# Rotary partners by on-chip copies, values in 64 columns and another order at the entry of an attention, on one core

## The chip, the core and the metric

The kernel runs on one core of one Trainium2 chip. The core has five engines, each with its own queue of instructions in a fixed order: TensorE (PE in the profile; its weight loads are PEld), VectorE (DVE), ScalarE (ACT), GpSimd (POOL) and SyncE (SP), which here only issues transfers (DMA). They meet at semaphores: an instruction waits until a counter has reached a value, and adds to one when it is done. The metric is the time of one execution in device microseconds.

## The reference

Two layers on `x` (32 rows of 64 tokens, 128 wide) and a context of the same shape. The change touches the first attention, and SyncE's part of the mixture of experts that follows it.

```python
# layer 0, attention: 16 heads of 8; query from layernorm(x), key and value from ctx
q = proj(query, Wq, bq); k = proj(key, Wk, bk); v = proj(value, Wv, bv)
q = q * cos + rotate_half(q) * sin          # rotate_half: [-x2, x1] inside a head
k = k * cos + rotate_half(k) * sin
attn_w = softmax(einsum('bhqd,bhkd->bhqk', q, k) * scale)
out = einsum('bhqk,bhkd->bhqd', attn_w, v) -> [B, S, D] @ Wo.T + bo
x = x + tanh(g_xattn[0]) * out
# layer 0, experts: per row of x the two best of 8 experts (128 -> 512 -> 128, gelu), weighted
x = x + tanh(g_ffn[0]) * moe(layernorm(x))
# layer 1: attention by autocorrelation (Fourier transforms), then a gated MLP in fp4 steps
```

## The kernel before

Everything stays in on-chip memory. The 2048 tokens are 16 tiles of 128 tokens (two rows of the batch each); four tiles make a group, so there are four groups of keys and four of queries. Every engine's program is written out by hand, in the order in which it runs. There is no scheduler: the order of the code and the semaphore waits alone set what runs when.

**Entry of the first attention** (before the loop over tiles). For each group, `project` multiplies 512 tokens by a weight matrix, and again by the same matrix with its columns exchanged (`wk0r`, `wq0r`): within a head of 8, channel i of the second result is channel i xor 4 of the first. This second one is the rotary partner. VectorE multiplies the one by the table `cos` and the other by `sin` while it reads them from PSUM (L837), and GpSimd adds the two (L384, semaphore `rope_sum`). So it goes for the four groups of keys and for queries 0 and 1. Queries 2 and 3 (`late_projection` on ScalarE, `late_queries` on GpSimd) are copied out of PSUM raw and turned on GpSimd. The queries come from layernorm(x): VectorE takes the statistics (L250, L257), GpSimd the power -1/2 (L282), ScalarE or VectorE normalises (L270, L272), TensorE turns a group over (`turn`, L1218) and ScalarE copies it into `xt` (L545). `values` makes the values in 8 rounds of 8 products with 128 columns each. Of the 128, ScalarE keeps the half that belongs to the heads on its partitions (L541).

The keys of a group are spread into 8 blocks `kbd`, one for each pair of heads, with all the other channels zero: a multiplication with a column of `hmask` for each block. Blocks of group 0 are made by VectorE (L844) and ScalarE (L560), those of group 1 by ScalarE, and those of groups 2 and 3 by GpSimd (L376).

**Loop over tiles.** On TensorE, step t is: turn the probabilities of tile t over (L1292), scores of tile t+2 (`keys_queries`, L1279), turn the output of tile t-1 over (L1311), weigh the values of tile t (`weigh_values`, L1305), project the output of t-1 (L1315). VectorE takes the maximum (L858) and subtracts it (L866); ScalarE copies the turned probabilities (L587), takes the exponent (L582), and copies the turned output (L592), which L1315 waits for. At t = 9 VectorE also takes the statistics of the first 8 finished tiles.

**Experts.** 64 pairs of row and expert are sorted by expert into 36 tiles: 28 with two pairs, then 8 with one. For each, SyncE reads the expert's number from on-chip memory (L338), waits until the buffer is free (there are six, so tile j waits for the second product of tile j-6), and issues the copy of that expert's weights from `wall` into the buffer (L341). TensorE then runs `hidden` (L1472) and `second` (L1487).

SyncE's queue begins with all the loads. The last of them, `ctxN` and `wall`, are first used after the attention.

## Time and profile before

| what | before |
|---|---|
| three runs: median, lowest, highest | 269.43, 267.22, 270.42 us |
| profiled execution: time, span | 268.33 us, 266.5 us |
| busy: PE, DVE, ACT, POOL | 247.3, 185.1, 162.8, 129.6 us |
| granted TensorE clock | 1.00 |
| first scores (L1279), first weighing (L1305) | 26.19 us, 35.08 us |
| end of the loop over tiles, experts | about 92 us, 105 to 169 us |

The span is from the first to the last instruction; the time has 1.83 us more around it. The profiled execution lies 1.10 us under the median of the three.

### The profile page before, as it was taken

The numbers are of one execution on the slowest core, as the hardware profiler recorded it, in microseconds if no ns is written. First come the engines' busy times: TensorE is split into PE (matmuls) and PEld (weight loads), VectorE is DVE, ScalarE is ACT, GpSimd is POOL, SyncE is SP. The second block draws the span as 40 slices with busy tenths as digits, with TensorE's granted clock in tenths as the row PEclk, the third lists the DMA queues.
The fourth block names the chain that finished last, engine by engine and source line by source line (L and its number), as shares of the span: only waits on it lengthen the run. The fifth ranks groups of instructions, "written<-read, shape, count | busy, mean of one in ns | idle before, by whom it ended". The sixth has DMA issues, their size and how long they took to land.

```text
span 266.5 us, 6458 instructions
## 1 busy us (share of the span) xinstructions
PE 247.3 (93%) x2290; PEld 189.4 (71%) x2290; DVE 185.1 (69%) x484; ACT 162.8 (61%) x384; POOL 129.6 (49%) x191
## 2 busy tenths in 40 slices
PE   7999999999989999999999997979899788899886
PEld 6655466667757886999999986756686454667675
DVE  4899588888889765253232232596578999999993
ACT  2469986655578654776656666574273787454542
POOL 4475579999520332224996111069055654352240
PEclk9999999999999999999999999999999999999999
DMA  6999100000000024977677776000000000000102
GB/s 184 379 340 409 60 4 2 0 4 2 2 2 1 2 86 186 370 315 302 277 301 290 288 296 240 2 1 0 2 1 0 0 2 0 0 20 21 42 22 59
DMA packets 12176, 30.10 MB, mean 113 GB/s; under 512 B 1008, under 2 KB 5232, under 8 KB 12016
## 3 DMA queue, kind: packets, MB, share of 16 engines
q1 hardware_dynamic: 12144, 29.69, 29.6%
q8 instruction: 18, 0.29, 0.4%
q14 instruction: 14, 0.11, 0.1%
HBM read 9.69 MB, written 1.05 MB: 40 GB/s over the span
## 4 chain that ended last, share of the span: by engine, by line
PE 57%; DVE 21%; issue 7%; ACT 6%; DMA 6%; SPq 1%; POOL 1%; DVEq 0%; ACTq 0%
PE ps L1472 9%; PE ps L1487 9%; PE ps L1305 6%; DMA s_region<-s_wall 5%; DVE s_region L306 4%; PE ps L1279 4%; PE ps L1292 4%; PE ps L1212 3%; DVE s_small L1144 3%; DVE s_region L1137 3%; PE ps L1615 3%; PE ps L1203 2%; PE ps L1315 2%; PE ps L1204 2%; DVE s_small L250 2%
## 5 line engine op out<-in xcount | busy, mean ns | idle before, releaser
L645 ACT ACTIVATE s_region<-ps,s_region 128x128 f32<-128x128 f32 (+1 forms) x144 | 39.4, 357 | 22.3 <-PE ps L1472 22.1
L996 DVE SCALAR_TENSOR_TENSOR s_ctxT<-ps,s_region,s_ctxT 128x64 f32 x64 | 16.4, 282 | 43.4 <-PE ps L1487 42.8
L1472 PE MATMUL ps<-s_region 128*128 128x128 f32 (+1 forms) x352 | 35.5, 259 | 2.6 <-DMA s_region<-s_wall 2.1
L1487 PE MATMUL ps<-s_region 128*128 128x128 f32 (+1 forms) x352 | 34.8, 256 | 0.2 <-DVE s_ctxT L996 0.2
L1472 PEld LDWEIGHTS ps<-s_region 128*128 128x128 f32 (+1 forms) x352 | 31.6, 172 | 4.4 <-DMA s_region<-s_wall 3.8
L1487 PEld LDWEIGHTS ps<-s_region 128*128 128x128 f32 (+1 forms) x352 | 31.6, 172 | 0.5 <-ACT s_region L645 0.3
L439 POOL COPY s_region<-s_xt 128x64 f32 x64 | 13.2, 234 | 32.9 <-PE ps L1472 24.3
L313 POOL TENSOR_TENSOR s_region<-s_region,s_small 128x704 f32<-128x704 f32 (+2 forms) x12 | 16.1, 1352 | 25.2 <-DVE s_region L306 25.2
L587 ACT COPY s_region<-ps 128x512 f32<-128x512 f32 x32 | 17.2, 592 | 16.2 <-PE ps L1292 16.2
L858 DVE TENSOR_REDUCE s_small<-ps 128x16 f32<-128x1024 f32 x16 | 19.6, 1224 | 9.4 <-PE ps L1279 9.4
L1671 PE MATMUL ps<-s_region 128*128 128x352 f32 x64 | 21.8, 470 | 4.1 <-ACT s_region L302 1.8
L376 POOL TENSOR_SCALAR s_region<-s_region 128x512 f32<-128x512 f32 x16 | 24.7, 1569 | 0.0
L280 POOL TENSOR_SCALAR s_small<-s_small 128x4 f32<-128x4 f32 (+3 forms) x14 | 3.3, 233 | 37.6 <-DVE s_small L257 37.6
L306 DVE SCALAR_TENSOR_TENSOR s_region<-s_region 128x704 f32<-128x704 f32 (+2 forms) x26 | 20.5, 794 | 0.8 <-ACT s_region L748 0.2
L1671 PEld LDWEIGHTS ps<-s_region 128*128 128x128 f32 x64 | 11.2, 189 | 11.2 <-DVE s_region L1137 2.9
L866 DVE TENSOR_TENSOR s_region<-ps,s_small 128x1024 f32<-128x1024 f32 x16 | 18.7, 1170 | 0.1
L1305 PE MATMUL ps<-s_region 128*64 128x18 f32 x512 | 17.8, 212 | 0.7 <-ACT s_region L587 0.6
L1305 PEld LDWEIGHTS ps<-s_region 128*64 128x64 f32 x512 | 16.2, 138 | 3.0 <-ACT s_region L587 1.3
L582 ACT ACTIVATE s_region<-s_region 128x1024 f32<-128x1024 f32 x16 | 17.2, 1074 | 1.1 <-DVE s_region L866 1.1
L1279 PE MATMUL ps<-s_region 64*64 64x512 f32 x128 | 17.4, 614 | 0.0
L1292 PE MATMUL ps<-s_par,s_region 128*128 128x128 f32 x128 | 16.7, 273 | 0.0
L282 POOL TENSOR_TENSOR s_small<-s_small,s_par 128x4 f32<-128x4 f32 (+3 forms) x14 | 15.8, 1131 | 0.0
(238 smaller groups left out, 521.7 us busy)
## 6 DMA issues: line engine op xcount, KB each, us to landing
s_region<-s_wall SPq DMA_DIRECT2D x36, 514.0 KB, 3.1
s_wall<-wall SPq DMA_DIRECT2D x8, 514.0 KB, 8.1
s_par<-par SPq DMA_DIRECT2D x1, 1258.0 KB, 10.8
s_x<-x SPq DMA_DIRECT2D x2, 512.0 KB, 7.3
out<-s_x SPq DMA_DIRECT2D x7, 128.0 KB, 1.8
s_region<-ffn SPq DMA_DIRECT2D x1, 560.0 KB, 3.6
s_ctxT<-ctxT SPq DMA_DIRECT2D x2, 256.0 KB, 4.1
s_ctxT<-ctxT SPq DMA_DIRECT2D x1, 512.0 KB, 7.2
```

The source lines that it names most:

```text
L306: return eng.scalar_tensor_tensor(out, mag, 1.5, z, ALU.max, ALU.subtract)
L376: pool.tensor_scalar(kbd[g % 2][:, j, :], cols, hmask[:, j:j + 1], None, ALU.mult).then_inc(m["kbd_done"], 1)
L582: act.activation(pr[t % 2], ssub[t % 2].rearrange("p h s -> p (h s)"), ACT.Exp, scale=scale).then_inc(m["exp_done"], 1)
L645: ins = act.activation(hg[j % 3][:, c, 0:n], ps[:, j % 3, n * c:n * (c + 1)], ACT.Gelu, bias=wbuf[j % 6][:, FF + FC * D + c:FF + FC * D + ...
L858: dve.tensor_reduce(mx[t % 2], scores(t % 2), AX, ALU.max).then_inc(m["mx_done"], 1)
L866: dve.tensor_tensor(ssub[t % 2], scores(t % 2), mx[t % 2].unsqueeze(2).broadcast_to([P, H, S]), ALU.subtract).then_inc(m["s_sub"], 1)
L1279: ins = mm(ps[S * row:S * row + S, 2 * (t % 2) + half, :], qT[rows, 2 * t + row, :], kbd[g % 2][rows, :, k:k + S], start=True, stop=True)
L1292: ins = tr(ps[:, 4 + half, P * k:P * k + P], pr[t % 2][:, c:c + P], ident)
L1305: ins = mm(ps[S * row:S * row + S, 6 + t % 2, n * c:n * c + n], pT[t % 2][:, c, S * row:S * row + S], vbd[:, 2 * t + row, c, :], start=Tru ...
L1472: ins = mm(ps[rows, j % 3, n * c:n * (c + 1)], w[:, P * c + rows.start:P * c + rows.stop], xg[j % 4][:, 0:n], start=True, stop=True)
L1487: ins = mm(ps[rows, 4 + j % 2, 0:n], w[:, lo + rows.start:lo + rows.stop], hg[j % 3][:, c, 0:n], start=(c == 0), stop=(c == FC - 1))
L1671: ins = mm(ps[:, 1 + 2 * n + t, 0:MLP], xqT[(q // 2) % 2][:, lo:lo + P], wguT[:, MT * P * n:MT * P * n + MLP], start=True, stop=True)
```

## The change

- **Partners by copies.** Only keys 0, keys 1 and queries 0 still have the second product. Of the other five groups (`SWAPS`: q1, k2, k3, q2, q3) TensorE makes one product, ScalarE writes it raw, with its bias, to its place (`raw_kept`), and SyncE issues 8 transfers of 16 partitions each, which copy it with channels i and i xor 4 exchanged into `other`. GpSimd then multiplies the two by the tables and adds them (`turn_raw`, three instructions).
- **Values with 64 columns.** 4 rounds of 16 products: each makes only the 64 columns that are kept.
- **Order at the entry.** x is loaded in three pieces (4, 4 and 8 tiles); statistics and normalising go in smaller parts, on GpSimd too (tiles 4 to 7 and 12 to 15); queries 2 and 3 come after the scores of tile 2. Blocks of keys are dealt out anew: of group 1 four by ScalarE, two by VectorE, two by GpSimd; of groups 2 and 3 four each by GpSimd and four by ScalarE, the latter inside the loop, at t = 3, 4, 5 and 7, 8, 9.
- **SyncE.** The 40 copies stand ahead of the loads of `ctxN` and `wall`. From tile 10 of the experts on, expert numbers are read ahead (two at every other tile), so that none is left to read from tile 27 on.

```diff
+            for i, name in enumerate(SWAPS):
+                sp.wait_ge(m["raw_kept"], i + 1)
+                for row in range(HD):
+                    sp.dma_start(other[i][row:P:HD], qk[name][(row ^ 4):P:HD]).then_inc(copied[i], 16)
             sp.dma_start(ctxN[:], a["ctx"].rearrange("(t u) s d -> (u s) t d", u=2)).then_inc(m["ld_ctxn"], 16)
...
+            def look_up(j):
+
+                s = TILE_SLOTS[j][0]
+                expert_of[j] = sp.value_load(experts[0:1, s:s + 1], min_val=0, max_val=E - 1)
...
             for j in range(MOE_TILES):
+                ahead = max(0, (j - 8) // 2)
+                while known < min(MOE_TILES, j + 1 + ahead):
+                    look_up(known)
+                    known += 1
                 feed(j)
...
+            def turn_raw(nth, name):
+
+                i = SWAPS.index(name)
+                pool.wait_ge(copied[i], 128)
+                for z, table in ((qk[name], "cos"), (other[i], "sin")):
+                    pool.tensor_tensor(z, z, pc(table).unsqueeze(1).broadcast_to([P, 8, S]), ALU.mult).then_inc(m["turned"], 1)
+                pool.wait_ge(m["turned"], 2 * nth)
+                pool.tensor_tensor(qk[name], qk[name], other[i], ALU.add).then_inc(m["rope_sum"], 1)
...
+            def raw_kept(name):
+
+                act.wait_ge(m["proj"], PROJECTED[name])
+                col = COL["bias0"][0] + (2 if name[0] == "k" else 0)
+                act.activation(qk[name].rearrange("p b s -> p (b s)"), ps[:, RAW_BANK[name], :], ACT.Identity,
+                               bias=par[:, col:col + 1]).then_inc(m["raw_kept"], 1)
...
             exponent(0)
-            late_projection(3)
-            key_blocks(1, 4, 6)
+            key_blocks(1, 0, 2, "kbd_second")
             for t in range(TILES):
                 probs_turned(t)
                 if t + 1 < TILES:
                     exponent(t + 1)
                 if t == 0:
-                    key_blocks(1, 6, 8)
+                    x_transposed(2)
+                    x_transposed(3)
+                    raw_kept(("q", 2))
+                    raw_kept(("q", 3))
+                    key_blocks(1, 2, 4, "kbd_second")
+                if t in (3, 4, 5, 7, 8, 9):
+                    j = t - 3 if t < 6 else t - 7
+                    key_blocks(t // 7 + 2, j, j + (1 if j < 2 else 2), "kbd_done")
                 if t >= 1:
                     output_turned(t - 1)
...
+            rope_products(0, ("k", 0))
+            dve.wait_ge(x_sem[0], 16)
+            ln_stats(dve, st, 0, 4)
+            rope_products(1, ("k", 1))
+            normalise(dve, 2, 4, m["xn_a_late"], 1)
+            dve.wait_ge(x_sem[1], 16)
+            ln_stats(dve, st, 4, 8)
+            masked_keys(0, 0, 3, "kbd_first")
+            rope_products(2, ("q", 0))
+            dve.wait_ge(x_sem[2], 16)
+            ln_stats(dve, st, 8, TILES)
...
             row_max(1)
+            normalise(dve, 8, 12, m["xn_a_late"], 3)
             subtract(1)
+            masked_keys(1, 4, 6, "kbd_second")
...
-                for k in range(4):
+                for k in range(8):
                     for half in range(2):
-                        ins = mm(ps[S * half:S * half + S, 4 + r % 2, D * k:D * k + D], ctxT[:, 4 * r + k, :], pc("wv0"),
-                                 start=True, stop=True)
+                        ins = mm(ps[S * half:S * half + S, 4 + r % 2, S * k:S * k + S], ctxT[:, 8 * r + k, :],
+                                 pc("wv0").rearrange("p (c h d) -> p h c d", h=2, d=HD)[:, half], start=True, stop=True)
```

TensorE, from the first projection to the first scores, before. L1203 and L1204 are a projection and its partner, L1212 the values, L1218 the turning of normalised tiles, L1279 scores:

```order
L1203 MATMUL ps<-s_ctxT,s_par 128x512
L1204 MATMUL ps<-s_ctxT,s_par 128x512
L1212 MATMUL ps<-s_par,s_ctxT 64x128 x16
L1218 MATMUL ps<-s_par,s_xn 128x128 x8
L1203 MATMUL ps<-s_xt,s_par 128x512
L1204 MATMUL ps<-s_xt,s_par 128x512
L1203 MATMUL ps<-s_xt,s_par 128x512
L1204 MATMUL ps<-s_xt,s_par 128x512
L1212 MATMUL ps<-s_par,s_ctxT 64x128 x16
L1218 MATMUL ps<-s_par,s_xn 128x128 x8
L1279 MATMUL ps<-s_region 64x512 x4
```

The same place in the changed kernel, up to the second block of scores. L1249 is a projection, L1251 a partner, L1260 the values, L1266 the turning, L1327 scores, L1338 the turning of probabilities:

```order
L1249 MATMUL ps<-s_ctxT,s_par 128x512 x2
L1266 MATMUL ps<-s_par,s_xn 128x128 x4
L1260 MATMUL ps<-s_par,s_ctxT 64x64 x16
L1249 MATMUL ps<-s_xt,s_par 128x512
L1251 MATMUL ps<-s_xt,s_par 128x512
L1266 MATMUL ps<-s_par,s_xn 128x128 x4
L1260 MATMUL ps<-s_par,s_ctxT 64x64 x16
L1249 MATMUL ps<-s_xt,s_par 128x512
L1327 MATMUL ps<-s_region 64x512 x8
L1338 MATMUL ps<-s_par,s_region 128x128 x8
L1327 MATMUL ps<-s_region 64x512 x4
L1266 MATMUL ps<-s_par,s_xn 128x128 x8
```

Five partner products are gone, the first scores stand after the turning of two groups instead of four, and the other two groups are turned behind the scores of tile 2.

ScalarE in the loop over tiles before, two steps. L587 copies turned probabilities, L582 is the exponent, L592 the copy of the turned output:

```order
L587 COPY s_region<-ps 128x512 x2
L582 ACTIVATE s_region<-s_region 128x1024
L592 COPY s_region<-ps 128x128
L587 COPY s_region<-ps 128x512 x2
L582 ACTIVATE s_region<-s_region 128x1024
```

The same engine in the changed kernel at t = 4 and 5. L620, L615 and L625 are the three of above, L591 a block of keys:

```order
L620 COPY s_region<-ps 128x512 x2
L615 ACTIVATE s_region<-s_region 128x1024
L591 ACTIVATE s_region<-s_region 128x512
L625 COPY s_region<-ps 128x128
L620 COPY s_region<-ps 128x512 x2
L615 ACTIVATE s_region<-s_region 128x1024
L591 ACTIVATE s_region<-s_region 128x512 x2
L625 COPY s_region<-ps 128x128
```

One or two blocks of keys now stand between the exponent of the next tile and the copy of the turned output.

SyncE at a single-pair tile of the experts before (every tile reads as this one):

```order
L338 TENSOR_LOAD s_small
L338 ISA x2
L341 ISA
L341 DMA s_region<-s_wall 128x1028
```

The same engine in the changed kernel, at the last tile that still reads expert numbers and the tile behind it; L351 is the reading, L357 the issue of the copy:

```order
L351 TENSOR_LOAD s_small
L351 ISA x2
L351 TENSOR_LOAD s_small
L351 ISA x2
L357 ISA
L357 DMA s_region<-s_wall 128x1028
L357 ISA
L357 DMA s_region<-s_wall 128x1028
```

The reading has gone from the last tiles and stands twice at every other tile from tile 10 on.

## Rows read from the trace of the kernel before

**Rows 1.** The page's head: span, and busy time of each engine.

```profile
span 266.5 us, 6458 instructions
PE 247.3 (93%) x2290; PEld 189.4 (71%) x2290; DVE 185.1 (69%) x484; ACT 162.8 (61%) x384; POOL 129.6 (49%) x191
```

**Rows 2.** Stretches: length, busy PE, PEld, DVE, ACT, POOL, granted clock, DMA share, GB/s.

```profile
26.00:35.08 9.08, 8.61 (x47) 3.47 (x45) 5.54 (x6) 9.06 (x17) 5.15 (x5) 1.00 0.19 76
35.08:67.40 32.32, 32.32 (x459) 22.15 (x461) 26.63 (x46) 21.16 (x38) 31.31 (x22) 1.00 0.01 2
```

**Rows 3.** Chain of waits at the entry: start, us, what ran.

```profile
7.10 1.90 PE ps L1212 x32
14.72 0.86 PE ps L1203 x2
...
27.15 2.44 ACT s_region L560 x4
29.59 1.16 ACT s_region L567 x2
...
35.08 1.11 PE ps L1305 x32
```

**Rows 4.** Groups by line and shape, stretch 0 to 75 (DVE 0 to 95): busy us, mean ns.

```profile
L858 DVE TENSOR_REDUCE s_small<-ps 128x16 f32<-128x1024 f32 x16 | 19.6, 1224 | 9.4 <-PE ps L1279 9.4
L866 DVE TENSOR_TENSOR s_region<-ps,s_small 128x1024 f32<-128x1024 f32 x16 | 18.7, 1170 | 0.1
L837 DVE SCALAR_TENSOR_TENSOR s_region<-ps,s_par 128x512 f32<-128x512 f32 x12 | 8.3, 741 | 0.7 <-PE ps L1204 0.7
L376 POOL TENSOR_SCALAR s_region<-s_region 128x512 f32<-128x512 f32 x16 | 24.7, 1569 | 0.0
L399 POOL TENSOR_TENSOR s_region<-s_region,s_par 128x512 f32<-128x512 f32 x4 | 5.0, 1278 | 2.9 <-ACT s_region L567 2.9
```

**Rows 5.** Timeline of the entry: start, us, engine, line, count.

```profile
8.90 1.65 DVE L250 BATCH_NORM_STATS2 s_small<-s_x 128x6 f32<-128x128 f32 x8 [0.35 <-DMA s_x<-x]
10.57 0.65 DVE L257 BATCH_NORM_AGGREGATE s_small<-s_small 128x2 f32<-128x6 f32 x8
...
13.68 3.19 ACT L270 ACTIVATE s_xn<-s_x,s_small 128x128 f32<-128x128 f32 x8
...
20.33 3.08 DVE L272 TENSOR_SCALAR s_xn<-s_x,s_small 128x128 f32<-128x128 f32 x8
...
26.07 1.07 ACT L545 COPY s_xt<-ps 128x512 f32<-128x512 f32 x2
26.19 1.09 PE L1279 MATMUL ps<-s_region 64*64 64x512 f32 x8
```

**Rows 6.** Timeline of one step of the loop (t = 2).

```profile
41.39 1.07 ACT L582 ACTIVATE s_region<-s_region 128x1024 f32<-128x1024 f32 x1
...
42.04 1.11 PE L1305 MATMUL ps<-s_region 128*64 128x18 f32 x32
42.35 0.27 ACT L592 COPY s_region<-ps 128x128 f32<-128x128 f32 x1
43.08 0.49 PE L1315 MATMUL ps<-s_par,s_region 128*128 128x128 f32 x2
```

**Rows 7.** Chain of waits at t = 9.

```profile
70.28 1.56 DVE s_small L250 x8
```

**Rows 8.** SyncE's issues of expert weights, whole kernel, and their landing.

```profile
L341 SPq DMA_DIRECT2D s_region<-s_wall x36: 485/486/565, 102.3 to 161.5; - x36
DMA to landing us min/median/max: 2.9/3.1/4.9
```

**Rows 9.** TensorE's waits by what ended them: us in total, times, longest.

```profile
PE ps L1537 <- ACT s_region L665: 1.4, 1, 1.4
```

**Rows 10.** Chain of waits in the last tiles of the experts.

```profile
155.32 4.84 DMA s_region<-s_wall
...
161.49 4.87 DMA s_region<-s_wall
```

More of the change, by code:

```diff
@@ L846, in _, with masked_keys @@
-                if r == 3:
-                    normalise(dve, TILES // 2, TILES, m["xn_a_late"], 2)
+            def masked_keys(g, first, last, done):
+                dve.wait_ge(m["rope_sum"], TURNED["k", g])
+                dve.wait_ge(m["hmask_ready"], 2)
+                for j in range(first, last):
+                    dve.tensor_scalar(kbd[g][:, j, :], qk["k", g].rearrange("p b s -> p (b s)"), hmask[:, j:j + 1], None,
+                                      ALU.mult).then_inc(m[done], 1)
@@ L1287, in turn_probs @@
                         pe.wait_ge(m["pt_done"], 2 * t - 1 + half)
-                    elif half == 0:
-                        pe.wait_ge(m["q_raw"], 2)
                     for k in range(4):
```

274 lines of the change are left out of this document (135 added, 139 removed).

## The prediction

> **What bounds the kernel now.** I read the page's head first: TensorE is busy 247.3 of 266.5 us [rows 1]. Busy is not bound, so I took the stretches that the change touches. From 26.0 to 35.1 us TensorE works 8.61 of 9.08 us, but ScalarE 9.06: the reader is to see that ScalarE is the full engine there. From 35.1 to 67.4 TensorE is busy 32.32 of 32.32 us, at a granted clock of 1.00: in the loop over tiles it is the bound, and whatever starts the loop earlier ends it earlier [rows 2]. The chain of waits says the same: values (1.90 us for two rounds) and projections (0.86 us for one product of 512 columns) on TensorE, then ScalarE's blocks of keys (2.44 us for four) and raw copies (1.16 us for two), until the first weighing of values starts at 35.08 us [rows 3]. That start is my measure of the entry. The first scores start at 26.19 us [rows 5].
>
> **TensorE's work ahead of the first scores.** Before, it is 6 pairs of products (12 x 0.86 = 10.3 us), 8 rounds of values (7.6) and 4 groups turned. I take 0.43 us for a group, half a product of 512 columns, since the transposes have 4 x 128 columns in place of 512 and the rows around them agree. Sum 19.6 us from 5.1 us on, and 1.4 us of waits give 26.2 [rows 3, 5]. After, it is 3 pairs (5.2), 3 single products (2.6), 2 groups turned (0.9) and 4 rounds of 16 products with 64 columns. No row shows that product over 128 channels at this place. The nearest is L1305: 16 products with the same 128x64 weights and 18 columns in 1.11 us. 64 columns can't be quicker, so a round costs at least 1.0 us; the other end is 16 products at what 16 cost before, 1.90 us [rows 3]. I take 1.1, near the row with the same weights, so 4.4 us for four rounds where there were 7.6. The sum is 13.1 us, so 18.2 us without waits.
>
> The waits: VectorE is through with keys 0 at 8.5 us and takes 1.4 for the statistics of 4 tiles (half of 1.65 and 0.65, and a short add), then 1.5 for the two products of keys 1, so 11.4. GpSimd's power is ready by then. Two tiles at 0.4 on ScalarE (3.19 for 8) and two on VectorE (3.08 for 8) let the first turning go at 12.9, some 0.3 us late. For tiles 4 to 7 VectorE's statistics end at 13.5, the power takes 1.5, and GpSimd normalises four at some 0.45 each, to 16.8. TensorE would be ready at 16.3, so this costs 0.5. Queries 0 leave TensorE at 16.1, VectorE at 17.6 and GpSimd (1.28) at 19.0. So the **first scores start at 19.1 us** in place of 26.19 [rows 4, 5].
>
> **From there VectorE is late next.** Its queue holds the statistics of the last 8 tiles (2.5 us) ahead of the first maximum, so that starts at 20.3. Maximum 1.2, subtraction 1.2, exponent 1.0: turned probabilities from 23.9 us, after a wait of TensorE of 2.7 us. VectorE goes on with the maximum of tile 1 (to 23.9), the newly placed normalising of four tiles (1.5) and the subtraction (to 26.6). ScalarE takes exponent 1 to 27.6, and only behind it the copies of the two turned groups (0.54 each): the first is there at 28.1. Then two projections (0.86 each, to 30.0), the raw copy of the last (0.6), the bias product that waits for it (two products of 128 columns, 0.8): the **first weighing starts at 31.6 us** in place of 35.08 [rows 3 to 6]. So 7 us of earlier scores become 3.5 us. The ends of the unknown costs: values at 1.90 us a round move it 1.3 us later (half of the 3.2 falls in VectorE's wait), pieces of x that land with the old 8.9 us move it 0.2 [rows 5], together -2.0 to -3.8 us.
>
> **ScalarE in the loop pays part of it back.** At t = 2 the copy of the turned output starts at 42.35 and takes 0.27; TensorE's L1315, which waits for it, starts at 43.08. ScalarE runs back to back from the exponent at 41.39 on, so there is a slack of 43.08 - 42.62 = 0.46 us, less some 0.04 for the semaphore [rows 6]. A block of keys is 0.61 us (2.44 for four) [rows 3], and the change puts one ahead of that copy at t = 3, 4, 7 and 8, two at t = 5 and 9. Behind the waiting L1315 stands the rest of TensorE's loop, which has no other idle time. One block costs 0.61 - 0.42 = 0.19, two cost 1.22 - 0.42 = 0.80. Four times 0.19 and once 0.80 is 1.6 us. The pair at t = 9 I count at nothing: there the chain is VectorE's, with its statistics at 70.28 us [rows 7], and if that cover is gone it costs 0.80 more. Net 3.5 - 1.6 = **1.9 us** at the end of the loop.
>
> **GpSimd and the copies, hidden if they are in time.** GpSimd has 10 blocks (1.57 each), 5 turnings of three instructions (3 x 1.28 = 3.8) and 4 additions of bias. In queue order: two blocks of keys 1 to 27.7 us, queries 1 to 31.5 (needed at 37.1 by the scores of tile 4), keys 2 to 37.2, four blocks to 43.5, queries 2 to 47.3 (needed at 53 by tile 8), keys 3, four blocks, queries 3 to 63.8 (needed at 69 by tile 12). Some 5 us are spare each time [rows 4]. For the copies: 40 issues in SyncE's queue, and behind them only `ctxN` and `wall`, which are used from 93 and 102 us on. An issue of 514 KB on SyncE takes 0.485 us and lands after 3.1 [rows 8]; eight are 3.9 us, so the five groups, the first of them raw at 19.7, are all there by 19.7 + 5 x 3.9 + 3.1 = 42.3 us. Nothing waits.
>
> Against this stands a rule of the Trainium skill (DMA: Bandwidth & Descriptors, Rules for kernel authors): transfers to disjoint sets of partitions share the same engines, so one transfer over 128 partitions is to be used instead; and its section on the anatomy of one DMA gives some 2.0 us fixed for each. If the 40 paid that one after the other, 80 us by that page, the fourth group would come at 84 us and the kernel would be over 30 us slower. What the rows of the weights show is that the fixed part of one transfer overlaps the next.
>
> **Experts.** In the last tiles the chain is made of landings of 4.84 and 4.87 us, where the median is 3.1 [rows 8, 10]. Both issues stand in the chain right behind TensorE's product that frees the buffer (155.2 and 161.4 us). So the reading of the expert number was over by then, and ahead of it there is nothing to win: 0.1 us, between 0 and 0.5. The double readings cost 1.5 us against a step of 1.8 and lie under a spare of over 2 us of landing. The removed instructions of TensorE move its code loads, which share the rings with these weights; that is +-1 us and unknown in sign.
>
> **Sum.** 268.33 - 1.9 - 0.1 = 266.3 us for the profiled execution (span 264.5). That execution lies 1.1 under the median of three; the middle of all four is 268.9, and I forecast 268.9 - 2.0 = **266.9 us**.
>
> **Rivals.** (1) *The blocks on ScalarE cost nothing*, since a block comes sooner behind the exponent than I count or TensorE's order has more slack: 268.9 - 3.6 = 265.3 us. For it speaks ScalarE's total of 21.16 of 32.32 us [rows 2], against it the back-to-back rows at t = 2. (2) *Copies late.* The place is the scores of tile 8, which need queries 2, the fourth group in SyncE's queue. With s us for one issue they are ready at 19.7 + 32 s + 2 + 3.8, and they are needed at 53: it decides from s = 0.86 on. At s = 1.0 all later tiles slip 4.9 us: 268.9 - 2.0 + 4.9 = 271.8 us, slower. For it: no row shows a transfer with 16 partitions, and a single receipt is not the median of a stream. Against it: 0.485 us with 36 samples, 0.565 at most [rows 8]. (3) *The clock falls.* TensorE's new wait of 2.7 us ahead of the first turned probabilities is longer than its longest before, 1.4 us, through which the clock stayed at 1.00, that is 2.4 GHz [rows 2, 9]. If it fell to 1.2 GHz until the first weighing, the TensorE work from there to the second weighing would double; replaced in the sequence above this is 5 us: 271.9 us. The Trainium skill (TensorE: Matmul & The Clock Gate, Part 1) says that idleness brings the throttled state back; no row here shows it happen after a wait. (4) *The gain is given back to landings in the experts*: 268.9 us, no change. The rows of 4.8 us show that these landings vary for reasons other than the issue.
>
> **Chances.** Forecast 0.52, blocks free 0.18, copies late 0.08, clock 0.07, given back 0.15. The forecast's own range is 265.3 to 268.3 us (entry 1.3 either way, code loads 1). 1% of this kernel, 2.7 us, is about what a measurement can tell from no change. Of the forecast some 0.19 lies beyond it, of the free blocks 0.16, and little of the rest: faster 0.36, slower 0.14 (2 and 3 with nearly all of their chance), same 0.50. The range from 264.6 to 269.8 leaves out the two slower cases and some 0.04 at the ends.
>
> **What would show it.** First scores at about 19 us, a wait of TensorE of some 2.7 us behind the second, first weighing at 31.6; in the steps t = 3, 4, 5, 7, 8 a wait of L1361 for L625, 0.2 us or 0.8; none for GpSimd at tiles 4, 8 and 12; expert issues right behind the products as before. I am wrong if the first weighing is not between 30.5 and 33, if the scores of tile 8 wait, or if the granted clock is not 1.00.

## The result, and the profile after

The changed kernel takes **269.25 us** (median of 12 runs, 268.46 to 270.70), the kernel before 268.28 us (median of 12, 267.18 to 270.42). The ratio is 1.0048, with a 95% interval from 1.0025 to 1.0070: 0.7 to 1.9 us slower. I had forecast 266.9 us, 2.0 us faster. 269.25 us lies in the range (264.6 to 269.8), but on the other side of no change. The profiled execution took 269.1 us, with a span of 267.3 against 266.5. Here and below a median is that of all executions, while a ratio leaves out the few that took over 1.5% longer than the fastest of their kernel.

The head of the page, and of its fourth part the line that shares out the chain of waits by line:

```profile
span 267.3 us, 6472 instructions
PE 242.4 (91%) x2280; PEld 185.5 (69%) x2280; DVE 181.0 (68%) x478; ACT 163.7 (61%) x376; POOL 132.4 (50%) x202
PEclk9998899999999999999999999999999999999999
SPq L351 7%; DMA s_region<-s_wall 6%; DVE s_region L312 4%; PE ps L1351 4%; PE ps L1338 4%; SPq L357 4%; PE ps L1517 3%; PE ps L1532 3%; PE ps L1327 3%; DVE s_small L1192 3%; DVE s_region L1185 3%; PE ps L1660 3%; ACT s_region L620 2%; PE ps L1249 2%; ACT s_region L615 2%
```

TensorE has 4.9 us less to do than in [rows 1], and the span is longer. Two things are new. The granted clock has two slices under full speed near the start, and the largest share of the chain is now L351, SyncE's reading of expert numbers. The milestones, taken from the timelines of TensorE:

| us from the start | before | forecast | after |
|---|---|---|---|
| first scores | 26.19 | 19.1 | 20.86 |
| first weighing | 35.08 | 31.6 | 33.92 |
| last weighing (tile 15) | 89.26 | 87.4 | 89.68 |
| first product of the experts | 105.37 | 103.5 | 105.89 |
| last product of the experts | 168.25 | 166.2 | 169.01 |
| span | 266.5 | 264.5 | 267.3 |

The miss of 2.8 us of span has its largest part at the entry: 2.3 us at the first weighing. The loop took what I had said: 55.76 us from the first to the last weighing, before 54.18, so 1.58 more. The remaining 0.5 us came in the experts and on the way to them.

**Entry.** Rows of the timelines (start, us, engine and line; in brackets the idle time before and what ended it):

```profile
8.25 1.12 PE L1249 MATMUL ps<-s_ctxT,s_par 128*128 128x512 f32 x2
9.21 1.02 PE L1251 MATMUL ps<-s_ctxT,s_par 128*128 128x512 f32 x2
...
10.16 1.15 PE L1260 MATMUL ps<-s_par,s_ctxT 128*64 128x64 f32 x32
...
11.36 1.27 ACT L575 COPY s_region<-ps 64x512 f32<-64x512 f32 x2 [1.65 <-PE ps L1260]
11.64 1.55 DVE L278 TENSOR_SCALAR s_xn<-s_x,s_small 128x128 f32<-128x128 f32 x2
11.76 1.35 POOL L402 TENSOR_TENSOR s_region<-s_region 128x512 f32<-128x512 f32 x1 [0.16 <-DVE s_region L875]
12.65 0.88 ACT L276 ACTIVATE s_xn<-s_x,s_small 128x128 f32<-128x128 f32 x2
13.63 0.63 PE L1266 MATMUL ps<-s_par,s_xn 128*128 128x128 f32 x4 [0.40 <-ACT s_xn L276]
...
14.42 0.17 DVE L266 TENSOR_SCALAR s_small<-s_small 128x4 f32<-128x4 f32 x1
...
16.29 1.74 POOL L278 TENSOR_SCALAR s_xn<-s_x,s_small 128x128 f32<-128x128 f32 x4
...
18.17 0.63 PE L1266 MATMUL ps<-s_par,s_xn 128*128 128x128 f32 x4 [0.91 <-DVE s_region L875]
...
20.86 2.03 PE L1327 MATMUL ps<-s_region 64*64 64x512 f32 x16
...
25.65 1.97 PE L1338 MATMUL ps<-s_par,s_region 128*128 128x128 f32 x8 [2.76 <-ACT s_region L615]
27.55 1.64 PE L1327 MATMUL ps<-s_region 64*64 64x512 f32 x8
```

A product of 512 columns takes 0.95 us from its start to the next (8.25, 9.21, 10.16) where I had 0.86. The round of values costs what I took: the next instruction, at 11.24, stands 1.08 us behind it. Two normalisings of VectorE took 1.55 us where I had 0.8: the first 0.34 us, the second 1.29, from 11.90 to 13.19 us, while GpSimd's addition L402 ran to 13.11. ScalarE normalises only from 12.65 us on, since its copy of the second round of values stands ahead. So the first turning starts at 13.63 instead of 12.9 us, the statistics of tiles 4 to 7 end at 14.6 instead of 13.5, and the second turning starts at 18.17 us. The view puts this wait down to L875, but GpSimd's normalising ends at 18.03 us: that came last. The wait of TensorE ahead of the first probabilities is 2.76 us as forecast (2.7), and what follows runs at half speed. Stretches of 1 us, where the number ahead of the last two is the granted clock:

```profile
24.00:25.00 1.00, 0.00 (x0) 0.00 (x0) 1.00 (x2) 0.56 (x2) 1.00 (x4) 1.00 0.22 64
25.00:26.00 1.00, 0.35 (x2) 0.35 (x3) 1.00 (x2) 1.00 (x2) 1.00 (x2) 0.65 0.12 35
26.00:27.00 1.00, 1.00 (x7) 1.00 (x6) 1.00 (x5) 1.00 (x3) 1.00 (x2) 0.50 0.23 66
27.00:28.00 1.00, 1.00 (x7) 0.52 (x10) 1.00 (x3) 0.73 (x2) 1.00 (x1) 0.50 0.15 43
28.00:29.00 1.00, 1.00 (x8) 0.00 (x0) 1.00 (x3) 1.00 (x2) 0.73 (x2) 0.64 0.22 64
29.00:30.00 1.00, 1.00 (x12) 0.86 (x8) 0.90 (x2) 0.48 (x2) 1.00 (x1) 1.00 0.19 55
```

From about 25.3 to 28.7 us the granted clock is 0.50, the level of 1.2 GHz, and then 1.00 again, which is 2.4 GHz. It fell while TensorE was still in its wait of 2.76 us.

**Loop.** First TensorE's waits for ScalarE's copy at t = 5 and t = 9, then SyncE's 40 copies (ns of one issue at least, in the median and at most; then who waited for them, and us to the landing):

```profile
53.95 0.49 PE L1361 MATMUL ps<-s_par,s_region 128*128 128x128 f32 x2 [0.73 <-ACT s_region L625]
...
69.59 0.49 PE L1361 MATMUL ps<-s_par,s_region 128*128 128x128 f32 x2 [0.73 <-ACT s_region L625]
```

```profile
L337 SPq DMA_DIRECT2D s_region<-s_region x40: 580/589/1903, 21.7 to 48.3; - x40
...
  POOL s_region L409: 0.3, 1
...
DMA to landing us min/median/max: 1.8/1.9/3.4
```

The copies let GpSimd wait once, for 0.3 us, at a place where nobody waits for it. The wait at t = 9 is as long as the one at t = 5, but it costs nothing, since TensorE then no longer waits for VectorE's statistics: of 1.6 us of such waits in the kernel before 0.2 are left.

**Experts.** The chain of waits from 126 us on, after. It shows two tiles; from 120 to 149 us it reads much the same, with SyncE alone in it:

```profile
126.44 0.48 SPq L357
126.97 0.27 SPq L351
127.27 0.15 SPq L351
127.61 0.49 SPq L357
128.14 0.55 SPq L351
128.72 0.15 SPq L351
128.97 0.86 SPq L351
129.86 0.15 SPq L351
130.21 0.49 SPq L357
```

Two tiles cost SyncE 130.21 - 126.44 = 3.77 us: two issues and three readings, of which the last of a pair takes 0.86. TensorE needs 4 x 0.89 = 3.6 us for two tiles (3.58 from start to start): in the chain of the kernel before, this stretch is made of TensorE's groups of products, and one of them reads

```profile
119.02 0.89 PE ps L1472 x8
```

So SyncE falls back by up to 0.19 us every two tiles. In the records of the trace this can be followed tile by tile: SyncE issues the weights of tile 8 0.12 us behind the product that frees their buffer (in the kernel before every tile from 8 on reads so, but for one at 0.22), those of tile 14 1.26 us behind it and those of tile 26 2.28 us. By then the spare of some 2 us between a landing and its use is gone. A landing stands in the chain that was not there before, ahead of the two of [rows 10]:

```profile
149.45 3.63 DMA s_region<-s_wall
...
157.08 4.85 DMA s_region<-s_wall
...
163.26 3.85 DMA s_region<-s_wall
```

and TensorE waits for it:

```profile
153.12 1.16 PE L1517 MATMUL ps<-s_region 128*128 128x128 f32 x8 [0.59 <-DMA s_region<-s_wall]
```

The readings themselves are longer than before. The first row is the kernel before, the second the changed one (ns at least, median, most):

```profile
L338 SPq TENSOR_LOAD <-s_small x36: 265/272/544, 101.4 to 160.4; - x36
```

```profile
L351 SPq TENSOR_LOAD <-s_small x36: 264/533/874, 101.8 to 148.2; - x36
```

### The profile page after: what moved, and what is told of

Same layout as the page of the kernel before. It is cut to its first block, busy times and chain, and to the rows that moved or that the text cites. A ratio compares the mean times of both kernels' runs of the same rounds, so it can differ in the third digit from the quotient of the medians.

```text
span 267.3 us, 6472 instructions
## 1 busy us (share of the span) xinstructions
PE 242.4 (91%) x2280; PEld 185.5 (69%) x2280; DVE 181.0 (68%) x478; ACT 163.7 (61%) x376; POOL 132.4 (50%) x202
## 4 chain that ended last, share of the span: by engine, by line
PE 40%; DVE 22%; SPq 11%; ACT 10%; issue 9%; DMA 7%; POOL 1%; DVEq 0%; ACTq 0%
SPq L351 7%; DMA s_region<-s_wall 6%; DVE s_region L312 4%; PE ps L1351 4%; PE ps L1338 4%; SPq L357 4%; PE ps L1517 3%; PE ps L1532 3%; PE ps L1327 3%; DVE s_small L1192 3%; DVE s_region L1185 3%; PE ps L1660 3%; ACT s_region L620 2%; PE ps L1249 2%; ACT s_region L615 2%
## 5 line engine op out<-in xcount | busy, mean ns | idle before, releaser
L1517 PEld LDWEIGHTS ps<-s_region 128*128 128x128 f32 (+1 forms) x352 | 31.6, 172 | 4.6 <-DMA s_region<-s_wall 3.9
L1532 PEld LDWEIGHTS ps<-s_region 128*128 128x128 f32 (+1 forms) x352 | 31.6, 172 | 0.5 <-ACT s_region L683 0.3
L473 POOL COPY s_region<-s_xt 128x64 f32 x64 | 13.2, 236 | 34.2 <-PE ps L1517 25.6
L620 ACT COPY s_region<-ps 128x512 f32<-128x512 f32 x32 | 17.3, 588 | 15.5 <-PE ps L1338 15.5
L906 DVE TENSOR_REDUCE s_small<-ps 128x16 f32<-128x1024 f32 x16 | 19.6, 1224 | 8.5 <-PE ps L1327 8.4
L1338 PE MATMUL ps<-s_par,s_region 128*128 128x128 f32 x128 | 17.6, 283 | 2.8 <-ACT s_region L615 2.8
L1327 PE MATMUL ps<-s_region 64*64 64x512 f32 x128 | 17.8, 633 | 0.0
L1338 PEld LDWEIGHTS ps<-s_par,s_region 128*128 128x128 f32 x128 | 15.1, 146 | 3.7 <-ACT s_region L615 3.6
L615 ACT ACTIVATE s_region<-s_region 128x1024 f32<-128x1024 f32 x16 | 17.1, 1068 | 0.8 <-DVE s_region L912 0.8
L288 POOL TENSOR_TENSOR s_small<-s_small,s_par 128x4 f32<-128x4 f32 (+3 forms) x15 | 16.4, 1096 | 0.0
```

The costliest lines, as they stand in the source:

```text
L615: act.activation(pr[t % 2], ssub[t % 2].rearrange("p h s -> p (h s)"), ACT.Exp, scale=scale).then_inc(m["exp_done"], 1)
L620: act.copy(pT[t % 2][:, 4 * half:4 * half + 4, :].rearrange("p a c -> p (a c)"), ps[:, 4 + half, :]).then_inc(m["pt_done"], 1)
L906: dve.tensor_reduce(mx[t % 2], scores(t % 2), AX, ALU.max).then_inc(m["mx_done"], 1)
L1327: ins = mm(ps[S * row:S * row + S, 2 * (t % 2) + half, :], qT[rows, 2 * t + row, :], kbd[g % 2][rows, :, k:k + S], start=True, stop=True)
L1338: ins = tr(ps[:, 4 + half, P * k:P * k + P], pr[t % 2][:, c:c + P], ident)
L1517: ins = mm(ps[rows, j % 3, n * c:n * (c + 1)], w[:, P * c + rows.start:P * c + rows.stop], xg[j % 4][:, 0:n], start=True, stop=True)
```

## The experiments

Three sets of four kernels; each set was measured with the kernel before on the same chip. All times are medians, with the ratio to that kernel before and its 95% interval.

### First set: the changed kernel with one edit each, and one part alone

**Expert numbers read one by one, as before.**

```diff
-                ahead = max(0, (j - 8) // 2)
+                ahead = 0
```

> The changed kernel, but each expert number is read right before its copy, as in the kernel before. Theory 1 (the loss lies in the entry and in ScalarE's blocks; the loop over tiles ends 0.4 us later than before): the experts take as long as before, 63.6 us from the first hidden product to the end, so 0.3 to 0.4 us less than in the changed kernel, and the whole gains 0.4 us at most. Rival (the double readings, up to 0.87 us each, bound SyncE from tile 10 on): 0.9 us or more is gained.

Measured: 268.70 us, 1.0029 [1.0006, 1.0053]. That is 0.5 us less than the changed kernel by the ratios, with intervals that overlap, and between the two theories (0.4 at most, 0.9 or more), so the times decide neither. The profile is clearer: SyncE's L351 has 2.2% of the chain from 118 to 170 us, where the changed kernel has 32.0%, and from 150 to 155 us TensorE is busy 5.00 of 5 us against 4.41. The last landing in the chain took 4.89 us against 3.85, and that ate the gain in this one execution: both spans are 267.3. It helps to cut the experts in two, at the first hidden product of a tile with one pair. The first row is the kernel before, the second the changed one:

```profile
155.13 0.69 PE L1472 MATMUL ps<-s_region 128*64 128x64 f32 x16
```

```profile
156.89 0.69 PE L1517 MATMUL ps<-s_region 128*64 128x64 f32 x16
```

From the first product of the experts to this one it is 49.8 us before, 51.0 in the changed kernel and 50.2 here: the single readings give 0.8 us back. The last eight tiles then took 12.1 us in the changed kernel and 13.1 both here and before.

**Blocks of keys behind the copy of the turned output.**

```diff
-                if t in (3, 4, 5, 7, 8, 9):
-                    j = t - 3 if t < 6 else t - 7
-                    key_blocks(t // 7 + 2, j, j + (1 if j < 2 else 2), "kbd_done")
                 if t >= 1:
                     output_turned(t - 1)
                 if t == TILES - 1:
                     tokens_turned(0)
+                if t in (3, 4, 5, 7, 8, 9):
+                    j = t - 3 if t < 6 else t - 7
+                    key_blocks(t // 7 + 2, j, j + (1 if j < 2 else 2), "kbd_first" if t > 6 else "kbd_done")
```

> The changed kernel with ScalarE's blocks of keys put behind the copy of the turned output instead of ahead of it, at the same steps t. If the blocks cost what the slack rows say, the steps t = 3, 4, 7, 8 become 0.19 us shorter and t = 5 0.80 us: the loop ends 1.6 us earlier, and the kernel is 1.6 us faster (267.7 against 269.3). Rival (a block in front of the next copy of probabilities costs as much there): no difference.

Measured: 268.05 us, 1.0015 [0.9987, 1.0043], 0.9 us less. From the first to the last weighing it is 54.18 us, exactly the kernel before, so the 1.58 us are back at the end of the loop. TensorE no longer waits there for L625. From the first to the last product of the experts it took 64.2 us, though, against 63.1 after and 62.9 before. This is no fault of the edit, nor of SyncE: up to the first tile with one pair it took 50.8 us, a little less than the 51.0 of the changed kernel, and the last eight tiles 13.3 against 12.1, with a last landing of 5.11 us.

**TensorE kept busy in its wait.** Three products of 512 columns, whose results nobody reads, stand in TensorE's queue behind the scores of tile 1:

```diff
             keys_queries(1)
+            pe.wait_ge(m["ld_rest"], 16)
+            pe.wait_ge(m["v_used"], 6)
+            mm(ps[:, 4, 0:512], ident, par[:, COL['wo0'][0]:COL['wo0'][0] + 512], start=True, stop=True)
+            mm(ps[:, 4, 0:512], ident, par[:, COL['wo0'][0]:COL['wo0'][0] + 512], start=True, stop=True)
+            mm(ps[:, 4, 0:512], ident, par[:, COL['wo0'][0]:COL['wo0'][0] + 512], start=True, stop=True)
```

> The changed kernel with three more products of 128x512 on TensorE behind the scores of tile 1 (2.6 us of work whose result nobody reads), in the wait for the first exponent. The clock should stay at 1.00, and the eight transposes and scores of tile 2 behind them take 1.1 and 1.1 us instead of 2.0 and 1.6. Theory 1: of these 1.5 us only 0.6 are gained, because the copies of the turned groups stand behind exponent 1, which starts at 28.2 us by VectorE. Rival: the full 1.5 us come back. If the clock is not what costs: nothing, or a loss.

Measured: 269.31 us, 1.0054 [1.0024, 1.0083]. No gain in time, but the clock does what the edit is for. TensorE, where the changed kernel had rows of 1.97 and 1.64 us:

```profile
24.51 1.02 PE L1391 MATMUL ps<-s_par 128*128 128x512 f32 x2
25.52 1.09 PE L1338 MATMUL ps<-s_par,s_region 128*128 128x128 f32 x8
26.54 1.09 PE L1327 MATMUL ps<-s_region 64*64 64x512 f32 x8
27.56 1.09 PE L1266 MATMUL ps<-s_par,s_xn 128*128 128x128 f32 x8
29.69 1.98 PE L1249 MATMUL ps<-s_xt,s_par 128*128 128x512 f32 x4 [1.04 <-ACT s_xt L579]
```

The last row says why a fall is cheap. At full speed TensorE is back at the queries early and then waits 1.04 us for ScalarE's copy L579, which stands behind the exponent of tile 1. In the changed kernel this wait is 0.24 us. From the first scores to the first weighing it is 12.43 us here and 13.06 after: **the fall costs 0.6 us**. The loop ended 0.8 us earlier than after, and the experts, still with double readings, took 63.9 us and gave it back (51.7 us up to the first tile with one pair).

**The kernel before with the reading ahead alone** (the `ahead` rule of the change, nothing else):

> The kernel before with nothing changed but the expert numbers read ahead. Theory 1: within 0.4 us of the kernel before, on the slower side. The rival of the first run (double readings bound SyncE): 0.9 us slower or more. If reading ahead helps the last tiles: faster by 0.1 to 0.5 us.

Measured: 269.17 us (7 runs), 1.0049 [1.0023, 1.0075]: 1.3 us slower. In its profile a landing of 3.88 us stands in the chain at 145.5 us, where the kernel before has TensorE alone. I had put this edit at 0.1 us of gain. This profile needs care: SyncE has 0.3% of the chain from 118 to 170 us, and the experts as a whole took 62.4 us, less than the 62.9 of the kernel before. But SyncE falls back as in the changed kernel (0.13 us behind the freed buffer at tile 8, 2.12 at tile 26), and up to the first tile with one pair it is 50.6 us against 49.8. The 0.8 us are lost there; the last eight tiles took 11.9 us against 13.1 and hide it.

### Second set: edits together, and the values alone

**The three edits of the first set together.**

> The changed kernel with the three repairs together: ScalarE's blocks behind the copy, three idle products in TensorE's wait, expert numbers read as before. Theory 1 (the losses add): the loop over tiles ends 2.2 us earlier than in the changed kernel and 1.8 us earlier than in the kernel before, and the kernel takes 1.5 to 2 us less than before. Rival (the experts end where the landings of their weights let them, whenever they start): the time stays within 0.7 us of before, and the experts take longer by what the loop gained.

Measured: 266.84 us, 0.9958 [0.9935, 0.9981], span 264.0. First weighing at 33.14 us, last at 87.32, 62.3 us for the experts, and TensorE has the chain there. The ratios of the three alone add up to 1.2 us less than the changed kernel; together it is 2.4 us. The intervals of the single runs are too wide to call this more than a sum. By the traces it is a plain sum: 1.6 us for the blocks in the loop and 0.8 us for the readings in the experts. The single profiles of these two edits hid it, since each met last tiles that were 1 us longer.

**Queries 0 earlier**: the same, with ScalarE's normalising ahead of its second copy of values, and GpSimd's additions put behind the powers and normalising, queries 0 ahead of keys 1.

```diff
             values_kept(0)
-            values_kept(1)
             normalise(act, 0, 2, m["xn_a"], 1)
+            values_kept(1)
...
             powers(pool, 0, 4)
-            sum_products(1, ("k", 1))
             powers(pool, 4, 8)
             normalise(pool, 4, 8, m["xn_a_pool"], 2)
             sum_products(2, ("q", 0))
+            sum_products(1, ("k", 1))
```

> As the run of the three repairs, and the way to the first scores is shortened: ScalarE normalises tiles 0 and 1 ahead of its second copy of values, and GpSimd adds queries 0 ahead of keys 1, so that it does not run beside VectorE's normalising. VectorE's two tiles should take 0.8 us instead of 1.55, and the first scores start at some 19.7 us instead of 20.9. Theory 1: 1.2 us less than the run of the three repairs, about 3 us less than before. Rival: another step is late at once, and less than 0.4 us is gained.

Measured: 267.06 us, 0.9935 [0.9913, 0.9958]. The first scores start at 19.77 us, against 20.72 in the run without this edit. With GpSimd's addition moved away, VectorE's two normalisings take

```profile
11.47 0.60 DVE L278 TENSOR_SCALAR s_xn<-s_x,s_small 128x128 f32<-128x128 f32 x2
```

in place of 1.55 us for both. The median is no lower than without the edit, the ratio 0.2% lower: the gain of 0.95 us is seen in the trace, not surely in the times.

**The same without the three products.**

> As the run with early queries, without the three idle products. The clock falls to half in the wait for the first exponent again, the transposes and scores behind it take 3.5 us instead of 2.1, and it is 0.6 us slower than with the products. Rival: the fall depends on how the wait lies, and the clock stays at 1.00 here, with no difference.

Measured: 266.05 us, 0.9927 [0.9903, 0.9952], span 264.1, clock 1.00 in this profile in spite of a wait of 2.76 us. The clock fell in 9 of the 12 runs all the same, so the expectation of a fall held and that of a loss did not: the products bring nothing that can be measured.

**The kernel before with values of 64 columns alone** (4 rounds of 16 products).

> The kernel before with the values in 4 rounds of 16 products with 64 columns, and nothing else. A round takes 1.1 us, so TensorE has 3.2 us less work ahead of its first scores. Theory 1: the first scores come some 1.5 us earlier (what is left is lost to waits for normalised tiles), but the first weighing only some 0.5 to 1 us, because ScalarE is full from 26 to 35 us. Rival: TensorE alone bounds the entry, and 3 us are gained.

Measured: 267.97 us, 0.9976 [0.9955, 0.9997], 0.6 us faster. First scores at 25.74 us, first weighing at 34.39, 0.7 us earlier than before. But 0.46 of these are an earlier landing of the first context in this execution (first projection at 4.69 us against 5.15). TensorE's rounds of values take 3.3 us less, and it waits 1.15 us for VectorE and 1.58 for GpSimd ahead of its first scores: without another order on the other engines the smaller rounds bring next to nothing.

### Third set: the readings again, and two questions left

The base of the first three is the kernel of 0.9927.

**Double readings put back.**

> The fastest version so far (expert numbers read one by one, blocks behind the copy, early queries, no products), with the changed kernel's reading of expert numbers ahead put back, and nothing else. Theory A (the two readings at every other tile cost more than the last tiles gain): slower than the version without them by what the same edit cost in the kernel before, 1.3 us, of which 0.5 would also do: ratio to before 0.995 to 0.998 in place of 0.9927. Theory B (the 1.3 us of that run and the 0.6 us of its counterpart were chance of where code loads fall): 0.991 to 0.994.

Measured: 267.59 us, 0.9958 [0.9922, 0.9993]. In its profile, one of its longest executions, the experts took 51.5 us up to the first tile with one pair.

**One reading ahead, never two together.**

```diff
-                ahead = 0
+                ahead = 1 if j >= 6 else 0
```

> The fastest version so far, with the expert number of the next tile read one tile ahead from tile 6 on: the same number of readings in each tile as before, never two together, but the reading no longer stands between the free buffer and the issue. Theory A (two readings together are what costs): no cost, 0.992 to 0.993, with at most 0.3 us gained. Theory C (reading ahead in itself costs, since it takes the reading out of SyncE's wait and puts the next one behind the issue): 0.995 to 0.998, as with two together.

Measured: **265.95 us, 0.9908 [0.9877, 0.9938]**, the fastest of all. The two kernels differ in this rule alone and stand 1.3 us apart, the same as the edit cost in the kernel before. The intervals overlap between 0.9922 and 0.9938. What shows it is that all traces agree, in the chain (SyncE has 48% of the stretch from 118 to 170 us with double readings and 0.1% here) and in the time from the first product of the experts to the first tile with one pair:

| kernels | reading | us |
|---|---|---|
| before; before with 64 columns | one by one | 49.8, 49.8 |
| before with readings ahead | double | 50.6 |
| six with the changed entry | one by one | 50.1 to 50.2 |
| this one | one ahead | 50.5 |
| changed; blocks behind; kept busy; double readings put back | double | 51.0, 50.8, 51.7, 51.5 |

Double readings cost 0.7 to 1.6 us in every trace. A reading here takes as long as before the change:

```profile
L351 SPq TENSOR_LOAD <-s_small x36: 266/270/832, 99.2 to 157.8; - x36
```

So reading ahead does little harm in itself: two readings together do. That it gains against reading in place (0.9927 in another set) is within the intervals.

**ScalarE's copies of the late queries ahead of the exponent of tile 1.**

```diff
+                if t == 0:
+                    x_transposed(2)
+                    x_transposed(3)
                 if t + 1 < TILES:
                     exponent(t + 1)
                 if t == 0:
-                    x_transposed(2)
-                    x_transposed(3)
                     raw_kept(("q", 2))
```

> The fastest version so far, with ScalarE's copies of turned groups 2 and 3 ahead of the exponent of tile 1 instead of behind it. Theory A (the first weighing waits for the chain copy, projection, raw copy, bias product, and the copies stand behind exponent 1): copies from 28.1 instead of 29.05 us, first weighing 0.9 us earlier (32.2 instead of 33.14), loop end and whole kernel 0.9 us earlier: 0.989 to 0.990. Rival (the exponent of tile 1, 1.1 us later, is what the second step waits for): the first weighing 0.9 us earlier, but a new wait of TensorE ahead of the second turning of probabilities, and no gain at the second weighing: 0.992 to 0.993.

Measured: 266.90 us, 0.9939 [0.9901, 0.9977]. Neither theory holds. In its profile the clock had fallen, the turning of the queries started at 28.13 us instead of 27.45, and the copies at 29.02: they waited 2.12 us for TensorE, not for the exponent. The first weighing came 13.2 us behind the first scores, as in the one-reading kernel, whose clock had fallen as well and which has the exponent first. With the clock down the edit had nothing to gain in this execution; what it does at full clock no profile here shows.

**Readings as before and blocks behind the copy, nothing else.**

> The changed kernel with two of the edits together: expert numbers read one by one as before, and the blocks of keys on ScalarE behind the copy of the turned output; no products in TensorE's wait, no other order of the queries. Theory A (the terms add up: 0.6 us for the readings, 0.9 for the blocks, by their single runs): 1.0048 less 0.0056 is 0.999. Theory B (by the profiles the blocks are worth 1.6 us, and their single run lost part of it in the landings of the experts, which the double readings made worse): 0.9965 or lower, near the 0.9958 of the run that had the products too.

Measured: 267.58 us, 0.9938 [0.9900, 0.9976]. The terms do not add up to 0.999: fixed together they give 2.9 us against the changed kernel, alone 0.5 and 0.9. The ratio agrees with theory B, but not with all of its reason: it is true that the single run of the blocks lost its gain in the landings of the experts, but it lost it in the last eight tiles, behind the double readings. The traces give 1.6 and 0.8, together 2.4 us. The interval is wide, since this set scatters more, and does not tell 2.4 from 2.9.

**How often the clock falls.** Mean granted clock of each run, counted where it is 0.994 or less:

| kernels | runs with a fall |
|---|---|
| before (three sets), before with 64 columns, before with readings ahead | 6 of 117 |
| changed kernel and all that keep the wait of 2.76 us | 70 of 95 |
| the three with products in the wait | 8 of 35 |

A mean does not say where the clock fell. Of the eight profiles of the middle row six show it at this wait. In the one profile of the last row with a fall, the clock is down from 176 to 179 us, behind another wait of 1.39 us, and not here. One fall of some 3 us to half costs the mean 1.5 / 267 = 0.006, which is the 0.994 of most of them; 13 of the 70 have 0.987 or less, and the two of these with a profile show a second such stretch, or one twice as long.

The six falls differ. In two the clock goes down within the wait, near its end, and in four only 0.2 to 1.5 us after TensorE has started again. With readings as before and blocks behind the copy it is down for nearly 7 us, from 24.9 to 31.7 us. Here the Trainium skill (TensorE: Matmul & The Clock Gate, Part 1) and the trace agree: idleness of this engine brings the throttled state back.

## Why the prediction was wrong

**The loop and the copies held.** I had a slack that leaves 0.19 us for one block and 0.80 for two, the pair at t = 9 hidden. The trace shows waits of 0.73 us for each pair and 1.58 us in all against my 1.6, and the edit that moves the blocks gives just that back. The copies cost 0.589 us an issue (I took 0.485) and landed after 1.9 us, and the next was issued before the last had landed. The rule against transfers over a part of the partitions (the Trainium skill, DMA: Bandwidth & Descriptors, Rules for kernel authors) decides nothing here, since only 0.3 us were waited. The 2.0 us that I took from its section on the anatomy of one DMA are given there for transfers that GpSimd issues; those of SyncE took 1.9. Rival 2 is out (its sum gives 4.5 us at s = 1.0, not 4.9); so is rival 1.

**The first step that failed is the sum for the first scores: 19.1 us forecast, 20.86 measured.** Of these 1.76 us, some 0.1 is the later landing of the first context. Some 1.2 us is the work term: 13.1 us forecast, and 14.3 in the trace (20.86 - 5.28 less the two waits), since nine products of 512 columns take some 0.95 us each, not 0.86, and a turning 0.56, not 0.43. The 0.86 of [rows 3] is a product between two others of its kind: in the timeline of before, four products and partners in a row start at 12.74, 13.70, 14.56 and 15.42 us and the values behind them at 16.37, so the first and the last take 0.96 and 0.95. In the new order nearly every product is a first or a last. I had the sum of before to test it with, and let "1.4 us of waits" take up the difference: its trace has one wait there, of 0.24 us, and 20.8 us of work where I had 19.6.

The last 0.5 us are waits: 0.40 and 0.91 us are in the rows, where I had 0.3 and 0.5. I counted ScalarE's two normalisings beside VectorE's, although its second copy of values (11.36 to 12.63) stands ahead of them. And two normalisings on VectorE at 0.8 us took 1.55: the second ended 0.08 us behind GpSimd's addition, which had started before it. My price came from the row of 3.08 us for eight [rows 5], and that row already held one such wait, spread over eight: in the trace of before seven of them take 0.33 us and one 1.29, to 21.87 us, beside an addition of GpSimd that ends at 21.78. Not every work of GpSimd does this: beside its blocks of keys (L398, from 25.36 us on) VectorE's four took 1.52 us. The run with early queries, without these two, has waits of 0 and 0.59 us there.

**The second is the clock.** I gave it a chance of 0.07 and a price of 5 us. It falls in three runs of four and costs 0.6 us in the changed kernel's profile. The chance was wrong, since I took a wait of 1.4 us without a fall as evidence for one of 2.7. The price was wrong, since I doubled TensorE's work up to the second weighing, where only the 3 us behind the wait ran slower, and more than half of that came out of a later wait for L579. The 0.6 us are no constant either: from the first scores to the first weighing it is 12.47 us in the profile without a fall of the same order (readings one by one), 12.85 where the fall came late and 14.14 where it lasted nearly 7 us, so 0.4 to 1.7 us. Of the forecast, 12.5 us for this stretch, 12.4 to 12.6 is what the profiles without a fall show.

**The third is the term "experts", -0.1 us.** "The double readings cost 1.5 us against a step of 1.8 and lie under a spare of over 2 us": the pair of readings fits into a step, but two tiles need three readings and two issues, 3.77 us against 3.58, and this holds for nine such pairs in a row, so it is a rate and uses up the spare of some 2 us. By the ratios it is 1.3 us in the kernel before and 1.3 in the fastest kernel, by the traces 0.7 to 1.6. The changed kernel's profile hides it: 0.24 us more than before, from the first to the last product of the experts, is all that it shows. That is 0.8 us for the double readings, 0.4 for something that all kernels with the changed entry have (a wait of 0.50 us at 108.8 us for the weights of an early tile, whose cause stays open), and 1.0 us less in the last eight tiles.

**The sum of the spans**: entry 2.3 us too good, experts 0.3, between the loop and the experts 0.1, the rest 0.1. That is the 2.8 us between 264.5 and 267.3. What came in truth is nearest to rival 4 (no gain, given back in the experts), with one difference: two thirds of the entry's gain were never there, and what took the rest back was, beside ScalarE's blocks, a rate of SyncE and not chance of the landings. That the time still lies in the stated range owes nothing to the forecast's own sum: it is the part of the range that was kept for rival 4.

**The last tiles.** The last eight tiles take 11.9 to 13.3 us in the traces at full clock, whatever the edit, and this alone decides how some of the profiles compare. I had put "+-1 us and unknown in sign" on code loads, and the size fits. They have a queue of their own, q8 in the profile, in packets of 16 KB; of its rows for the kernel before, from 150 to 168 us:

```profile
q8 instruction: 2, 0.03, 0.9%
```

One of the two packets starts at 157.0 us, inside the landing of 4.84 us, the other at 162.6, inside that of 4.87. In the changed kernel the second one starts only at 166.4, when the last landing (3.85 us, to 167.1) is nearly over. Over all 14 traces, without the first six tiles of each, 127 transfers of weights had such a packet start while they were under way and took 3.97 us in the median; the 129 that had none, nor one in the 6 us before, took 2.93. Of the 51 landings of more than 4.4 us 43 are of the first kind, and 7 were issued within 2 us of such a packet. This is agreement in time: no run here moves the code loads and nothing else.

## What to carry to other kernels

A queue that only issues transfers has a rate of its own. Add up everything it does in one period, register reads included, and compare it with the period of the engine it feeds: nine pairs of tiles at up to 0.19 us each were enough here to use up a spare of 2 us. Work that is moved ahead should be spread evenly, one piece a period.

An early milestone is worth only as much as the next limit behind it lets through. Ask of each earlier start what stands ready for it on every engine, in that engine's queue order. And compare stretches of several traces, not whole spans: two edits gave 2.9 us together and 1.4 as a sum by their ratios, but 1.6 and 0.8 us in the stretches that they touch, and the rest lies within the intervals.

A mean duration is a poor price. The row of eight normalisings looked like 0.39 us each and was seven of 0.33 and one of 1.29; the product of 0.86 us was one from the middle of a row.

A block of work on a helper engine costs nothing behind the result that others wait for, and its full length, less the slack, ahead of it: 1.58 us here, and nothing.

## What the runs showed of the hardware

- A reading of a register from on-chip memory on SyncE takes 0.27 us where SyncE waits between tiles. Where issues and single readings follow each other without a pause it is mostly 0.48 to 0.54 us (the kernel before, 103 to 113 us), and of two together the first mostly takes 0.55 and the second 0.86 us.
- VectorE's two normalisings of 128x128 took 1.55 us with a GpSimd addition of 1.35 us beside them, 0.60 without. The whole difference is in the one that started behind the addition: it ended with it.
- A landing of 514 KB of weights takes 2.93 us in the median where no 16 KB code load falls into it or just before it, and 3.97 where one does.
- With a wait of TensorE of 2.76 us in the kernel, 70 of 95 runs show a fall of the clock, in six of eight profiles at this wait, to half for some 3 us or twice that. The fastest kernel shows a second fall, at the end of the experts: its last landing takes 5.59 us in the chain, and from 165 to 168 us the granted clock is 0.50:

```profile
165.00 1.12 PE L1517 MATMUL ps<-s_region 128*64 128x64 f32 x16 [1.18 <-DMA s_region<-s_wall]
165.90 2.72 PE L1532 MATMUL ps<-s_region 128*64 128x64 f32 x48
...
```

- Forty transfers of 16 partitions inside on-chip memory: 0.589 us an issue, 1.9 us to the landing, overlapping.
